# Order of the tiles in a sparse graph-attention layer: group 1 first, its tiles one a step, and the query projections spread over steps 0 to 2

## The reference

```python
mask = adj.astype(float32) + eye(n)
q, k, v = (h @ Wq.T + bq), (h @ Wk.T + bk), (h @ Wv.T + bv)      # each (n, 8, 32)
scores = einsum('nhd,mhd->hnm', q, k) / sqrt(32)
attn = softmax(where(mask == 0, -1e9, scores))
ctx = einsum('hnm,mhd->nhd', attn, v).reshape(n, 256)
h1 = layer_norm(h + ctx @ Wo.T + bo, ln1_g, ln1_b)
ff = relu(h1 @ W1.T + b1) @ W2.T + b2                            # 1024 wide
h2 = layer_norm(h1 + ff, ln2_g, ln2_b)
```

## Time and profile before

| | us |
|---|---|
| median of 3 runs (549.91 to 551.04) | 550.61 |
| the profiled execution, its own time | 551.84 |
| its span, first to last instruction | 549.6 |
| TensorE busy (products) | 481.0 (88%) |
| VectorE busy | 386.3 (70%) |
| GpSimd busy | 278.4 (51%) |
| ACT busy | 219.5 (40%) |

### The profile page before, as it was taken

The page is one execution under the profiler, slowest core; times in us unless marked ns, Lnnn a source line. Parts: engine busy times, 40 slices in busy tenths (PEclk is TensorE's granted clock), DMA queues, the critical chain, the costliest instruction groups (busy, mean ns, idle before and its releaser), DMA issues.

```text
span 549.6 us, 7512 instructions
## 1 busy us (share of the span) xinstructions
PE 481.0 (88%) x2328; PEld 376.4 (68%) x2328; DVE 386.3 (70%) x1067; ACT 219.5 (40%) x547; POOL 278.4 (51%) x384
## 2 busy tenths in 40 slices
PE   5999998947447999999999999999987799989993
PEld 4888887736324786687588588478745588868782
DVE  0558876477922889899899899697777578966103
ACT  1233352323313246236524633733463436254530
POOL 7555342432700466686786644445464556771202
PEclk9999998965767999999999999998999999999998
DMA  7999969979993689999999937718267484430001
GB/s 178 294 270 270 261 235 193 317 243 131 245 223 128 134 184 227 150 240 173 234 229 160 231 133 146 146 59 161 91 114 145 133 167 140 143 99 20 20 1 42
DMA packets 43132, 92.20 MB, mean 168 GB/s; under 512 B 4936, under 2 KB 21192, under 8 KB 42960
## 3 DMA queue, kind: packets, MB, share of 16 engines
q0 software_dynamic: 16512, 55.60, 52.3%
q1 hardware_dynamic: 24784, 34.22, 17.9%
q10 hardware_dynamic: 1792, 1.85, 1.0%
HBM read 123.61 MB, written 16.80 MB: 255 GB/s over the span
## 4 chain that ended last, share of the span: by engine, by line
PE 59%; issue 10%; DVE 8%; DMA 6%; ACT 5%; POOL 5%; SPq 5%; POOLq 0%; ACTq 0%; DVEq 0%
PE ps L1129 16%; PE ps L1142 15%; PE ps L1861 10%; SPq L1522 4%; PE ps L1109 3%; PE ps L876 3%; DMA row_be<-in_be 2%; PE ps L1097 2%; PE ps L879 2%; POOL slots L1042 1%; DMA work<-q_table,row_of 1%; POOL slots L1052 1%; DMA early<-in_wqkvT 1%; PE ps L891 1%; ACT early L1193 1%
## 5 line engine op out<-in xcount | busy, mean ns | idle before, releaser
L1129 PE MATMUL ps<-xT_all,w 128*128 128x512 f32 (+1 forms) x320 | 122.4, 529 | 16.8 <-DMA w<-in_w1T 9.1
L1142 PE MATMUL ps<-w,xT_all 128*128 128x256 f32 x512 | 117.3, 382 | 3.1 <-ACT xT_all L1183 2.2
L1142 PEld LDWEIGHTS ps<-w,xT_all 128*128 128x128 f32 x512 | 94.9, 190 | 15.4 <-ACT xT_all L1183 2.7
L1129 PEld LDWEIGHTS ps<-xT_all,w 128*128 128x128 f32 x320 | 59.3, 196 | 59.8 <-issue 36.1
L1052 POOL DMA_INDIRECT slots<-kv_table,col_of x54 | 55.6, 1030 | 86.1 <-DVE col_of L620 69.5
L1183 ACT ACTIVATE xT_all<-ps,col_table 128x512 f32<-128x512 f32 (+1 forms) x80 | 47.8, 602 | 73.9 <-PE ps L1129 71.4
L1042 POOL DMA_INDIRECT slots<-kv_table,found x48 | 50.4, 1050 | 41.6 <-PE ps L879 25.1
L1861 PE MATMUL ps<-early,xT_all 128*128 128x256 f32 x256 | 59.6, 394 | 6.1 <-DMA early<-in_wqkvT 6.1
L1861 PEld LDWEIGHTS ps<-early,xT_all 128*128 128x128 f32 x256 | 50.0, 198 | 13.9 <-DMA xT_all<-in_xT 4.7
L1060 POOL DMA_INDIRECT work<-q_table,row_of x40 | 44.7, 1117 | 15.6 <-issue 14.1
L531 DVE MAX8 adj_bytes<-adj_bytes 128x8 f32<-128x1024 f32 (+5 forms) x40 | 38.2, 973 | 19.0 <-DMA adj_bytes<-in_adj 19.0
(11 more groups left out here) (180 smaller groups left out, 862.6 us busy)
## 6 DMA issues: line engine op xcount, KB each, us to landing
adj_bytes<-in_adj POOLq DMA_DIRECT2D x31, 512.0 KB
kv_table<-slots POOLq DMA_DIRECT2D x7, 1024.0 KB, 14.4
xT_all<-in_xT SPq DMA_DIRECT2D x13, 512.0 KB, 30.9
slots<-kv_table SPq DMA_DIRECT2D x12, 512.0 KB
q_own<-q_table SPq DMA_DIRECT2D x12, 256.0 KB
out_dram<-early SPq DMA_DIRECT2D x6, 512.0 KB
slots<-in_adj SPq DMA_DIRECT2D x1, 2048.0 KB, 24.3
q_table<-slots SPq DMA_DIRECT2D x8, 256.0 KB
```

What stands on the lines that cost most here:

```text
L1129: last = nc.tensor.matmul(ps[:, q["bank"] + f % 2, 0:q["g"] * P], w1[:, k, f * P:(f + 1) * P], q["h1T"][:, k, :], start=(k == 0), stop=(k ...
L1142: nc.tensor.matmul(to, q["ffT"][:, f, j * P:(j + 1) * P], w2[:, f, :], start=(f == 0), stop=False)
```

## The change

Group 1 (tiles 4 to 7) becomes the first group, so steps 0 to 3 are single tiles, steps 4 to 15 are the pairs, and steps 16 to 18 are tiles 1 to 3 as before. Four query pairs are projected ahead of step 0 and twelve in steps 0 to 2, four a step. The first job starts in step 4 (`FIRST_JOB`) and not in step 2. Seven jobs are whole, and only group 0 is two half jobs. SP issues w1, w2, row_g and row_be at the end of step 1, behind wo. Tile 0's pieces move two steps later, its sum one step. GpSimd loads four adjacency tiles before step 0 and no more until step 1; then two a step. The idle products are gone.

```diff
-ORDER = [5, 6, 4, 3, 2, 7, 1, 0]
+ORDER = [1, 5, 6, 4, 3, 2, 7, 0]
...
-GATHER0, SCORE0 = 2, 4
+GATHER0, SCORE0 = 4, 6
...
-SUM0 = NB - 3
-
-SINGLES = min(q.b for q in STEPS if q.T == 1)
-WIDE_JOBS = STEPS[SINGLES].group
+SUM0 = NB - 2
+
+LATE = NB - 3
+WIDE_JOBS = STEPS[LATE].group
+FIRST_JOB = min(q.b for q in STEPS if q.group == 1)
...
-        for g in ORDER[WIDE_JOBS:]:
-            JOBS.append(job(2, GROUP * g, 0, POST, main))
-            JOBS.append(job(2, GROUP * g + 2, 2, POST, main))
+        JOBS.append(job(2, GROUP * ORDER[-1], 0, POST, main))
+        JOBS.append(job(2, GROUP * ORDER[-1] + 2, 2, 0, post_signals("e_")))
...
-        Q_BEFORE, Q_LISTS = 9, 6
+        Q_BEFORE, Q_LISTS = 4, 2
 
         def q_pairs(i, gap):
-            if i == 0:
-                return ((9,), (10,), (11, 12), (13,), (), ())[gap]
-            return ((14,), (15,), (), (), (), ())[gap] if i == 1 else ()
+            at = Q_BEFORE + GROUP * i + gap
+            return (at,) if gap < GROUP and at < PAIRS else ()
...
         def late_ff(i, gap):
 
-            return {(S, 4): (W, (0, 1)), (S + 1, 1): (W, (2,)), (S + 1, 2): (W, (3, 4)), (S + 1, 3): (W, (5, 6)), (S + 1, 4): (W, (7,)),
-                    (S + 3, 0): (A1, (0, 1, 2)), (S + 3, 1): (A1, (3, 4)), (S + 4, 2): (A1, (5, 6, 7)),
-                    (S + 5, 2): (A2, (0, 1, 2, 3)), (S + 5, 3): (A2, (4, 5, 6, 7))}.get((i, gap), (0, ()))
+            return {(S, 4): (W, (0, 1)), (S + 1, 1): (W, (2,)), (S + 1, 2): (W, (3, 4)), (S + 1, 3): (W, (5, 6)),
+                    (S + 1, 4): (W, (7,))}.get((i, gap), (0, ()))
 
         def late_out(i, gap):
 
-            return {(S, 2): (W - 1, (2,)), (S, 3): (W - 1, (3,)), (S + 2, 2): (W, (0,)), (S + 2, 3): (W, (1,)),
-                    (S + 3, 2): (W, (2,)), (S + 3, 3): (W, (3,)), (S + 4, 3): (A1, (0,)), (S + 5, 0): (A1, (1,)),
-                    (S + 6, 1): (A2, (0,)), (S + 6, 2): (A2, (1,))}.get((i, gap), (0, ()))
+            return {(S, 2): (W - 1, (2,)), (S, 3): (W - 1, (3,)), (S + 2, 0): (W, (0,)), (S + 2, 1): (W, (1,)), (S + 2, 2): (W, (2,)),
+                    (S + 2, 4): (W, (3,))}.get((i, gap), (0, ()))
...
-                if i == 2:
+                if i == FIRST_JOB - 1:
                     load_own(sp, TILE0)
...
                 if i == 1:
                     sp.dma_start(wo[:], woT.rearrange("(k p) n -> p k n", p=P)).then_inc(s_wo, 16)
-                if i == 2:
                     sp.dma_start(w1[:], w1T.rearrange("(k p) n -> p k n", p=P)).then_inc(s_w1, 16)
                     sp.dma_start(w2[:], w2T.rearrange("(k p) n -> p k n", p=P)).then_inc(s_weights, 16)
                     for name, src in (("g2", g2), ("be2", be2)):
                         sp.dma_start(rows[name][:], src.to_broadcast([P, D])).then_inc(s_weights, 16)
...
-                if 3 <= c < 5:
-                    load_adj(pool, 1 + c)
...
-                if i + 3 < NB and i != 1:
+                if 0 < i < NB - 3:
                     load_adj(pool, STEPS[i + 3].h)
-                if i == 0:
-                    load_adj(pool, STEPS[3].h + 1)
...
-                if i == 2:
+                if i == FIRST_JOB:
                     pe.wait_ge(s_q, PAIRS)
-                if i == 3:
+                if i == FIRST_JOB + 1:
                     pe.wait_ge(s_weights, 16 * WEIGHT_DMAS)
...
-                if i in (S + 1, S + 5):
-                    idle_product_pe(pe, 1)
...
-                if S < i < NB - 1:
-                    idle_product_pe(pe, 2 if i == S + 1 else 1)
...
-                    idle_product_pe(pe, 3)
```

More of the change, by code:

```diff
@@ L909, in tr0_pe @@
             last.then_inc(psum0, 1)
[L911 to L916, removed]
         def sum0_pe(pe, k):
@@ L1161, in post_act_h1 @@
             last.then_inc(q["h1T_done"], 1)
[L1163 to L1168, removed]
         def post_act_h1_bias(act, q, n):
             act.wait_ge(q["h1T_done"], n + 1)
-            halves_free(act, q, n)
+            wait(act, q["out_ps"], n)
             for k in range(KC):
@@ L1414, in apart, with ff_gap, outs_own @@
             return step_of_job(q)[1] == 1 and finished(q) >= 0 and q.b + 2 < NB and STEPS[q.b + 2].T == 1
-        def count_of(g):
-            return len([p for p in STEPS if p.group == g])
-        Q_BEFORE, Q_LISTS = 9, 6
+        Q_BEFORE, Q_LISTS = 4, 2
         def q_pairs(i, gap):
-            if i == 0:
-                return ((9,), (10,), (11, 12), (13,), (), ())[gap]
-            return ((14,), (15,), (), (), (), ())[gap] if i == 1 else ()
[L1429 to L1441, removed]
+            at = Q_BEFORE + GROUP * i + gap
+            return (at,) if gap < GROUP and at < PAIRS else ()
+        def ff_gap(place, gap):
+            return (((), (), (), (), (), (0, 1)), ((2,), (3, 4), (5, 6, 7), (), (), ()))[place][gap]
+        def outs_own(place, gap):
+            return {(1, 3): (0, 1)}.get((place, gap), ())
         def outs_before(place, g, gap):
@@ L1503, in _ @@
                     load_own(sp, STEPS[i + 1])
-                if i != 1:
-                    for gap in range(6):
-                        for p in q_pairs(i, gap):
-                            store_q(p)
-                if i == 2:
+                for gap in range(6):
+                    for p in q_pairs(i, gap):
+                        store_q(p)
+                if i == FIRST_JOB - 1:
                     load_own(sp, TILE0)
-                if place == 1 and q.group <= WIDE_JOBS:
+                if place == 1:
                     if q.group == 0:
@@ L1543, in _ @@
             c = JOBS[LAST]
-            for n in (A1, A2, B1):
+            for n in (W, B1):
                 post_store(sp, JOBS[n], n, JOBS[n]["t"])
@@ L1661, in _ @@
                     gather_edges(pool, TILE0, (2 * (i - GATHER0), 2 * (i - GATHER0) + 1))
[L1662 removed]
+                if place == 0 and n >= 1:
                     post_pool_rstd(pool, JOBS[n - 1], n - 1, 1)
[L1664 to L1667 removed]
+            a, b, c = JOBS[W], JOBS[B1], JOBS[LAST]
+            na, nb, ne = W, B1, 0
             post_pool_rstd(pool, a, na, 1)
@@ L1742, in dense @@
                     if n >= 0:
-                        post_act_ff(act, now, n, ff_gap(place, count, gap))
+                        post_act_ff(act, now, n, ff_gap(place, gap))
                 if i > 0:
@@ L1913, in dense @@
                     if n >= 0:
-                        post_pe_ff(pe, now, n, ff_gap(place, count, gap))
-                        post_pe_out(pe, now, n, outs_own(place, count, gap))
-                if i == 2:
+                        post_pe_ff(pe, now, n, ff_gap(place, gap))
+                        post_pe_out(pe, now, n, outs_own(place, gap))
+                if i == FIRST_JOB:
                     pe.wait_ge(s_q, PAIRS)
-                if i == 3:
+                if i == FIRST_JOB + 1:
                     pe.wait_ge(s_weights, 16 * WEIGHT_DMAS)
@@ L1935, in _ @@
                 dense(2)
+                if i == WEIGHTS0:
+                    tr0_pe(pe)
                 tr_pe(pe, q)
@@ L2044, in _ @@
             rt_dve(dve, TILE0)
-            find_dve(dve, STEPS[2], 1)
             cols_dve(dve, TILE0)
```

127 lines of the change are left out of this document (29 added, 98 removed).

## The result

The changed kernel takes 568.55 us (median of four runs, 568.33 to 570.58) where the kernel before, run beside it, takes 550.83: a ratio of 1.030 (1.026 to 1.034). The forecast was 552.3, with a range of 538 to 561. "Slower" had a chance of 0.50, but 18 us slower was in no case of the forecast. The profiled execution has a span of 566.6 us; the mean granted clock fell from 0.949 to 0.924.

What follows compares the result with a forecast made beforehand. TensorE bounds the paired steps, while DMA engines are busy 0.84 of the early stage. Terms sum to 541.4 against 540.7 (+0.7), plus 1 for the single steps' period: 552.3 us by the median, range 538 to 561.

Steps and rivals of the forecast that it cites:

- Step 3's stall: VectorE waits 14.5 us for step 3's own rows, queued behind the weights and landing at 151; step 3 ends at 165.
- ceiling: Latest landing of step 3's own rows: 154 us, taking 38 us as from w1 to row_be in the kernel before.
- weights through early: Rival: own rows land by 137, no stall in step 3, 14.5 us less, total 538; chance 0.22.
- the DMA engines stretch the single steps too: Rival: gathers of steps 2 and 3 queue behind adjacency tiles, 18 us a step, +4 to +9, total 559; chance 0.20.
- The clock stays up: Rival: step 0 starts at 84 and queries keep TensorE at work, up to 3 us for the chunks; total 546; chance 0.16.
- Steps 4 and 5: First steps with a job, repeating the old steps 2 and 3 with two chunks at low clock: 49.5 us.
- Steps 14 and 15: Two paired steps at 44.0 us, plus tile 0's transposed weights, less two score pieces: 46 us.
- Step 16: What old step 12 takes, 22.4, less 3.2 for tile 0's products, a little more for three units: 20 us.
- the 30 us that the old late stage loses: TensorE loses some 30 us in old steps 12 to 18, idle products counted; about 1 us a step after the change.
- Step 17: Late single step with eight chunks, tile 0's sum and small products: 23.7 us of work, 25 with waits.
- step 18: Last step, with four second-layer tiles, half an attention and the rest: 21 us.
- the tail: From last sum to last product: 33.6 us before, 2 more for the last second-layer tile and normalizing operations, 35.6.

Runs made afterwards that it cites:

- e1: Changed kernel with step 3's own rows issued in step 1 ahead of w1, w2, row_g and row_be on SP's queue: 568.74 us, ratio 1.030.
- e5: Changed kernel with w1, w2, row_g and row_be issued at 62 us, behind the first query pair's store: 559.71 us, ratio 1.012.
- e4: Changed kernel with nine idle products in TensorE's idle times in steps 13, 14 and 16: 564.02 us, ratio 1.022.
- e2: Changed kernel with tile 0's score pieces, softmax and transposed weights two steps later, its sum in step 17 as before: 558.58 us, ratio 1.008.
- e8: Changed kernel with GpSimd working out the job's first norm in step 16 ahead of the three gathers: 562.27 us, ratio 1.019.
- e3: Changed kernel with step 3's own rows ahead of the weights and tile 0's pieces two steps later: 557.32 us, ratio 1.010.
- e6: Changed kernel with weights issued at 62 us and tile 0's pieces two steps later: 547.82 us, ratio 0.991.
- e11: Kernel before the change without its eleven idle products: 556.46 us, ratio 1.009.
- e7: Kernel before the change with w1, w2, row_g and row_be issued right behind the first query pair's store: 537.78 us, ratio 0.971.
- e10: Changed kernel with weights at 62 us, tile 0's pieces two steps later, and norms ahead of gathers in steps 4 and 16: 547.13 us, ratio 0.993.
- e12: Changed kernel with early weights, later tile 0, norms ahead in steps 4 and 16, and ten idle products in step 3: 547.76 us, ratio 0.991.

## Why the prediction was wrong

**Step 3's stall: right in kind, mis-sized.** The own rows landed at 157.5 us and not at 151. The sum of bytes by the old rate was 6.5 us short (from 117 to 157.5 us the software queue took 26.6 us' worth of full DMA engines where the forecast had 22.9, and SP's queue 14.7 where it had 11.8), and the 154 that the forecast called its ceiling was passed: the 23.7 us of the earlier trace rows became 27.05. The start and the periods were near: edge scores at 86.5, 104.8, 120.3 and 139.4 for 87, 102.5, 118 and 135. The rival "weights through early" did not come: the DMA engines were busy 0.98 of the time or more from 102 to 157 us. Its premise (from a landing before 149 each us is one us of the total) depends on how the rows get there early. In e1 only their place in the queue changed; step 3 ended 16.7 us earlier and the total did not move. In e5 the bytes left the stretch, and step 3's 10.5 us came back as some 10 in the total. The wait belongs to the bytes in the crowded stretch, not to one load. In e1 step 3's own rows, issued ahead of the weights, were there in time, and those issued behind were late. The Trainium skill (DMA: Bandwidth & Descriptors, Queues, rings and completion order) has the ring consumed in order; by that rule, the trace agrees, in both orders.

Of the other rivals, "the DMA engines stretch the single steps too" held in part: the periods are 18.3, 15.4 and 19.1 us, and VectorE waits 3.5 us for gathered queries in step 3. "The clock stays up" did not: step 4 has 0.67 (from 170.2 to 190.7 us).

**Steps 4 and 5: 4.5 us too long in the forecast.** It kept 6.2 us for two chunks at half clock. Step 4 did run at low clock, but by the time the chunks came the clock was back; two took 3.4 us, and only the first of the attention, the eight transposes and the step's sum were slow. That this error cancelled the one before is luck.

**Steps 14 and 15: the step of the forecast that failed.** It took the 44.0 of two paired steps, added tile 0's transposed weights and took off two score pieces. It moved TensorE's work only. With the new numbering tile 0's softmax, which stood in step 11 beside the search of one single tile, stands in step 13 beside the searches of two, and VectorE, "not far behind" by the forecast's own first paragraph, reached the head of step 14 too late for TensorE. The price of 8.6 us has three parts, by estimate: about 4 us more in which TensorE had nothing, 3 of low clock behind it (e4 gets 3.1 back), and 1.7, half of the 3.4 us at half clock behind the 28 products. e2 moved the softmax and these products and gave 44.7. That the softmax passes are what delays VectorE is read from its timeline; e2 moves more than them.

**Step 16: failed in the same manner.** "What step 12 takes, 22.4, less those 3.2" took the 28 products for work on the path. They were the cover of a norm: with them gone TensorE waits 6.1 us for what GpSimd works out behind three gathers, and then runs at half clock. e8 shows the cause (GpSimd's order), since the step then takes 19.7; in e3 and e6, where the products stand there again, TensorE waits 0.4 us for the norm.

**The idle products were not free to go.** The forecast counted them into the 30 us that the old late stage loses, and so into the gain. In the kernel before they are worth 4.7 us (e11), by holding the clock at 1.00. The late stage of the changed kernel lost them and gained new waits; e4 gets 4.4 us back with nine of them.

**Step 17, step 18, the tail** came to +1.1, -2.6 and +2.3, 0.8 together. The +2.3 of the tail was not tried.

Added up: against the 18 us over the kernel before, the runs show 12 that go with tile 0's place (e2), of which part is clock, and 10 that go with the weights (e5); the kernel before has a loss of some 15 us of its own at the weights (e7), so this second loss isn't the change's alone. With both repaired the changed order (e6) is still 10 us behind the old order with early weights (e7). By the pages of these two, e6 has 6.1 us more of products (472.5 against 477.6 less the 11.2 of idle products, as in the earlier trace rows) and 2.3 more of the rest of the span (72.2 against 69.9). So low clock is most of what remains. It is not the step in which the first job starts: e6 has 0.66 there (step 4, 157.2 to 178.8 us), but e7 has 0.66 too (step 2, 132.3 to 153.2). The windows that differ are others: from 60 to 80 us e6 has 0.84 and TensorE busy 14.4 us, where e7, with more query pairs ahead, has 1.00 and 18.9; step 3 of e6 has 0.51 and step 16 0.93. No run removed this, and whether the early single steps could be had without it stays open.

## What to carry to other kernels

When a renumbering moves work, re-sum every engine for each step, not only the bound one: find where a long piece of the second-busiest engine (here 6 us of softmax passes) meets its other long pieces, and ask of each product that leaves a gap what it was covering. The wait behind the full queue wasn't removed by reordering that queue; look for a stretch where the bytes hold up nobody. That was worth some 15 us to the kernel that nobody meant to change (e7, the fastest here), even with the DMA engines already busy 0.84 of that stretch. And price a new wait of TensorE above its length: what runs behind it may run at half clock for some us.

## What was not expected of the hardware

A short VectorE operation of two SBUF operands (L548, 0.22 us at its median) took 2.25 us in step 13, from 394.26 to 396.51, while GpSimd's addition of two SBUF operands ran from 394.03 to 396.44: VectorE's ended just behind it. About 2 us of the 5 that TensorE idled there are this. The meeting itself isn't new: the same pair of operations meets four times in every trace of the changed order and three times in each of the old one, 53 times in all, each time with about 2.25 us and an end just behind GpSimd's. It costs where TensorE waits for it; in step 13 of e2 (392.64) it costs nothing. The Trainium skill (SBUF — State Buffer, SBUF: two separate sides) says that the two engines' shared ports are locked for a whole instruction, also for a VectorE operation with two SBUF inputs; by this rule, the trace agrees.

The clock fell in step 16 of e2 behind a wait of 1.96 us. From 446 to 450 us it is 0.50, with TensorE busy throughout. In e6 the same step has the same products and a wait of 2.0 us, and keeps 1.00 at that point:

```profile
446.00:450.00 4.00, 4.00 (x16) 3.44 (x15) 2.57 (x12) 0.77 (x4) 0.95 (x1) 0.50 0.46 132
```

```profile
435.00:439.00 4.00, 4.00 (x27) 3.43 (x26) 3.14 (x17) 1.96 (x6) 1.55 (x2) 1.00 0.46 135
```

Five runs have this step with the same late order and a wait of 1.95 or 1.96 us. In e2 and e10 the clock falls within 2 us behind the wait, in e3, e6 and e12 it doesn't; in all five it falls near the end of the 28 products. So the same schedule can run at either clock, worth 4 us in this step (28.3 against 24.1); a forecast has to carry both.
